# Row sums of the attention weights with queries on partitions, their reciprocals on VectorE, in a decoder layer on one core

## Chip, cores and metric

The kernel runs on 1 core of one Trainium2 chip. The metric is device time in microseconds, the median of three runs. One launch computes the whole layer: an attention with distance weights, a cross attention, and a mixture of experts.

## What is computed

Only the first of the three parts is touched. For each of 2 batches and 16 heads, with 1024 tokens and 64 columns per head (cut to what matters):

```python
P = X @ W_in + b_in                                  # X is the normalised input
Q, K, V, G = jnp.split(P, splits, axis=-1)
W = jnp.power(EPS + _cdist(Q, K), -P_POW)            # EPS = 1e-4, P_POW = 2
W = W / (EPS + jnp.sum(W, axis=-1, keepdims=True))   # the row sums
A = jnp.einsum('hbts,hbse->hbte', W, V)
H = G * A
return H @ W_out + b_out
```

The cross attention and the experts follow on `x + attention`.

## The kernel before, in words

The attention goes through 16 **pairs** of two heads (8 pairs for each batch). Weights of a pair lie in `wts` as [128 keys, head, 8 blocks of keys, 1024 queries]: keys on partitions, queries in the free dimension. The engines run one software pipeline that is written out by hand; each engine has its own program and waits on counting semaphores. In pair p:

- **TensorE** goes through 8 blocks of keys. Block b has `values(p, b)` (weights times V into `ps_o`, L593), a slice of `project_qk(p + 2)` (L488 into `ps_p`, from block 1 on), and `distances(p + 1, b)` (L577 into `ps_s`). `ps_s` has room for one block, so each `distances` waits until VectorE has taken the block before it. After the blocks come `project_v` and `project_g` of the next pair (L488), `turn_v` (8 transposes, L552), `row_sums(p)` (L606) and `norm_k(p + 2)` (L523, 8 matmuls of 2 columns).
- **VectorE** adds the first two blocks of weights into `acc_w` (`add_first`, L1027), and then has for each block `guard` (distances out of PSUM into `wts`, L1046) and `add_second` (the second head's sum, L1035). In between are the copies of q and k. The end of the pair has `copy_values`, `copy_vt`, `step_k`, `split_high`, `copy_v`, `split_low` (L1020 to L997), `copy_k2` (L1001) and `copy_g` (L1010). The first `distances` of the next pair waits for the last two.
- **ScalarE** takes the square roots of the next pair (`roots`, L1580), and then logarithm and exponential of the blocks (`weights`, L1586 and L1588), which give distance to the power of -2.
- **GpSimd** adds the first head's blocks (`add_block`, L1782) and splits weight matrices for the projections.

**Row sums before.** `acc_w` holds, for each head, the sum over the blocks, still with 128 keys on partitions. `row_sums` multiplies by a matrix of ones with 64 columns, so that `ps_p` gets the row sum of every query on the 64 partitions of its head: 4 matmuls of 512 columns. ScalarE takes `rinv = exp(-ln(sum + eps))` in two passes over 1024 columns (`rows_log` L1568, `rows_inverse` L1572), put between the chunks of the next pair's `weights`. GpSimd multiplies G by it (`gate_rows`, L1788), and VectorE multiplies the values by that product (`gate`, L1064).

In the last pair there is nothing to prepare, and TensorE runs `context()` ahead of the values: keys and values of the cross attention (L471 and L479, 80 records of few columns). VectorE has its own `context()` behind `add_first`. After the last pair, SyncE loads the input again, the output weights (both into the room of `wts`) and the first tile of heads, and TensorE begins `attn_out` (L666).

Of the kernel before, what the change touches and what calls it, by code (L numbers as in the profile page):

```python
# [108 lines left out]
def program(nc, x, ctx_t, mask, w_in, b_in, w_out, w_x, b_cols, rows_in, gate_w, w1, w2, w3, consts, r_consts, out):  # L109
    with ExitStack() as ctx:  # L110
# [46 lines left out]
        rinv = sb("rinv", [P, T])  # L157
        q32, k32, v_t = qk, norms, qk_sq
# [83 lines left out]
        def h_part(j, n):  # L242
# [42 lines left out]
                 "v_ok", "max_ok", "h_ok", "sqq_ok", "sqk_ok", "add0_ok", "add_ok", "addb_ok", "gr_ok", "sqrt_ok", "ln_ok", "w_ok", "rln_ok", "r_ok", "h_out",  # L285
# [161 lines left out]
        def _(pe):  # L447
# [45 lines left out]
            def project_qk(p, i0, i1, rows_before):  # L493
                for i in range(i0, i1):
                    if i == 0:
                        pe.wait_ge(S_.wqk_ok, 2 * p + 2)
                        if isinstance(p, int) and p == 1:
                            pe.wait_ge(S_.vt_ok, 1)
                        if rows_before is not None:
                            pe.wait_ge(S_.rln_ok, rows_before)  # L500
                    if i == STEPS:
                        pe.wait_ge(S_.q_ok, p + 1)
                    mm = project_step(ps_p, wqk_hi, wqk_lo, p, i // STEPS, i % STEPS)
                    if i == STEPS - 1:
# [91 lines left out]
            def row_sums(n, turned):  # L596
                pe.wait_ge(S_.add_ok, NA * (n + 1))
                pe.wait_ge(S_.addb_ok, NA * (n + 1))
                if turned:
                    pe.wait_ge(S_.vt_ok, n + 2)  # L600
                else:
                    pe.wait_ge(S_.rln_ok, n)
                for th in range(2):
                    t = slice(th * HALF, (th + 1) * HALF)
                    for h in range(2):
                        mm = pe.matmul(ps_p[h * DH:(h + 1) * DH, t], cst[:, C_ONES:C_ONES + DH], acc_w[:, h, t], start=True, stop=True)  # L606
                mm.then_inc(S_.sum_mm, 1)

            def pair(p, first=False, ahead=2):

                if ahead == 0:
                    context()
                for b in range(SB):
                    values(p, b)
                    if ahead == 2:
                        project_qk(p + 2, QK_STEPS[b], QK_STEPS[b + 1], None if first else p)
                    if ahead >= 1:
                        distances(p + 1, b)
                if ahead >= 1:
                    if ahead == 1:  # L620
                        pe.wait_ge(S_.rln_ok, p)
                    project_v(p + 1, p + 3 if ahead == 2 else PAIRS)
                    project_g(p + 1, ps_s[:, 1])
                    turn_v(p + 1)
                row_sums(p, ahead >= 1)
                if ahead == 2:
                    norm_k(p + 2, ps_s[:, 0])
# [25 lines left out]
            pair(PAIRS - 1, ahead=0)  # L653

# [48 lines left out]
            def turn_p(i, g, n):  # L703
                if g <= 1:
                    pe.wait_ge(S_.exp_ok, 3 * i + 2 + g)
                if g == 0:
                    if n == 0:
                        pe.wait_ge(S_.rln_ok, PAIRS)
# [208 lines left out]
        def _(dve):  # L917
# [141 lines left out]

            def gate(n):  # L1060
# [38 lines left out]
            def pair(p, first=False, ahead=2):  # L1099

                if ahead >= 1:
# [23 lines left out]
                if ahead == 2:  # L1125
                    split_low(p + 2)
                    copy_k2(p + 2)
                if ahead >= 1:
                    copy_g(p + 1)

# [32 lines left out]
            pair(PAIRS - 1, ahead=0)  # L1163
            dve.wait_ge(S_.x2_in, 16)
# [373 lines left out]
        def _(act):  # L1538
# [25 lines left out]
            def rows_log(n):  # L1564
                act.wait_ge(S_.sum_mm, n + 1)
                if not (isinstance(n, int) and n == 0):
                    act.wait_ge(S_.gr_ok, n)
                act.activation(rinv[:], ps_p[:], ACT.Ln, bias=eps_d[:, 0:1]).then_inc(S_.rln_ok, 1)  # L1568

            def rows_inverse(n):  # L1570
                act.wait_ge(S_.rln_ok, n + 1)
                act.activation(rinv[:], rinv[:], ACT.Exp, scale=-1.0).then_inc(S_.r_ok, 1)  # L1572

# [8 lines left out]
            def weights(n, first):  # L1582
                act.preload_act_table_set("natural_log_exp_and_others")  # L1583
                for c, (start, end) in enumerate(LOGS):
# [153 lines left out]
        def _(pool):  # L1738
# [85 lines left out]
            gate_rows(PAIRS - 1)  # L1824
# [122 lines left out]
```

## Time and profile before

| what | value |
|---|---|
| median of 3 runs | 1432.39 us (1429.56 to 1433.23) |
| the profiled execution: its own time | 1428.5 us |
| its span | 1426.4 us |
| TensorE busy | 1263.9 us, 89% |
| VectorE busy | 1132.7 us, 79% |
| ScalarE busy | 1036.4 us, 73% |
| GpSimd busy | 708.7 us, 50% |
| ScalarE, logarithm and exponential of the weights (L1586, L1588) | 246.0 and 238.4 us |
| VectorE, guards (L1046) | 296.9 us |

The busy time of an engine is the sum over its instructions, and engines overlap. The attention fills the first 22 of the page's 40 slices, about 800 us. In nearly all of these ScalarE and TensorE stand at 9 tenths or more, so the average over the whole span says little: what a change in the attention is worth is read from one of its pairs.

### The profile page before, as it was taken

What the parts mean: (1) busy time and instruction counts of PE and PEld (TensorE: products, weight loads), DVE (VectorE), ACT (ScalarE), POOL (GpSimd) and SP (SyncE); (2) the same over time, 40 slices, a digit from 0 to 9 for tenths busy, and PEclk for the clock granted to TensorE, in tenths of its full rate; (3) what the DMA queues carried; (4) which work ended last, traced back from release to release, by engine and by line L of the source; (5) the groups of instructions that cost most, each with busy time, mean ns of one, the idle gap of its engine ahead of it and who ended that gap; (6) DMA issues with size and microseconds to landing.
All of it is one profiled execution on the core that took longest, in us unless ns stands there. A gap on an engine that the chain in (4) does not pass through costs nothing.

```text
span 1426.4 us, 23505 instructions
## 1 busy us (share of the span) xinstructions
PE 1263.9 (89%) x7513; PEld 865.1 (61%) x7513; DVE 1132.7 (79%) x1569; ACT 1036.4 (73%) x839; POOL 708.7 (50%) x524
## 2 busy tenths in 40 slices
PE   5899999999999999999998955999993699999992
PEld 4545554554455455545544714888873599999992
DVE  7988998898889889888988473788886867777771
ACT  1699999999999999999999931333332356666661
POOL 5456656665665666566655152333330245565642
PEclk9999999999999999999999767999995799999996
DMA  5000000000000000000000124222220134334422
GB/s 156 5 11 16 30 15 29 15 22 22 15 29 15 29 15 29 15 29 15 15 22 0 28 76 130 85 67 66 66 98 15 31 91 123 76 97 98 101 30 74
DMA packets 69214, 67.78 MB, mean 48 GB/s; under 512 B 6816, under 2 KB 61600, under 8 KB 69152
## 3 DMA queue, kind: packets, MB, share of 16 engines
q1 hardware_dynamic: 61504, 56.91, 12.6%
q0 software_dynamic: 7680, 10.49, 4.4%
q8 instruction: 17, 0.28, 0.1%
q14 instruction: 13, 0.11, 0.0%
HBM read 49.29 MB, written 20.19 MB: 49 GB/s over the span
## 4 chain that ended last, share of the span: by engine, by line
PE 35%; ACT 19%; issue 19%; DVE 13%; DMA 7%; POOL 5%; POOLq 1%; DVEq 0%; ACTq 0%; SPq 0%
ACT wts L1586 11%; PE ps_s L577 8%; DMA acc<-norms,tok_put 6%; PE ps_o L593 6%; PE ps_o L666 4%; ACT wts L1588 4%; DVE wts L1046 3%; PE ps_p L488 3%; PE ps_o L879 2%; PE ps_s L699 2%; PE ps_s L727 2%; PE ps_s L846 2%; POOL head_rows L1864 2%; ACT L1583 1%; POOL tok_now L1861 1%
## 5 line engine op out<-in xcount | busy, mean ns | idle before, releaser
L1782 POOL TENSOR_TENSOR v_aug<-v_aug,wts 128x1024 f32<-128x1024 f32 x96 | 232.4, 2421 | 227.3 <-DVE v_aug L1035 226.9
L1046 DVE TENSOR_SCALAR wts<-ps_s,k 128x1024 f32<-128x1024 f32 x240 | 296.9, 1278 | 55.3 <-PE ps_s L577 51.9
L593 PE MATMUL ps_o<-wts,head_rows 128*64 128x512 f32 x1024 | 249.0, 610 | 3.6 <-ACT wts L1588 3.6
L1586 ACT ACTIVATE wts<-wts,eps_d 128x2048 f32<-128x2048 f32 (+1 forms) x96 | 246.0, 2562 | 0.2
L1580 ACT ACTIVATE wts<-wts 128x4096 f32<-128x4096 f32 (+1 forms) x80 | 230.1, 2931 | 21.0 <-DVE wts L1054 18.6
L1588 ACT ACTIVATE wts<-wts 128x2048 f32<-128x2048 f32 (+1 forms) x96 | 238.4, 2483 | 3.0
L577 PE MATMUL ps_s<-q_hi,k_hi 64*128 64x512 f32 x512 | 122.5, 471 | 34.0 <-DVE wts L1046 17.8
L593 PEld LDWEIGHTS ps_o<-wts,head_rows 128*64 128x64 f32 x1024 | 63.2, 137 | 128.0 <-issue 118.0
L1035 DVE TENSOR_TENSOR v_aug<-v_aug,wts 128x1024 f32<-128x1024 f32 x96 | 126.5, 1317 | 6.6 <-ACT wts L1588 6.2
L577 PEld LDWEIGHTS ps_s<-q_hi,k_hi 64*128 64x128 f32 x512 | 49.3, 185 | 103.4 <-DVE wts L1046 62.5
L577 PE MATMUL ps_s<-q_lo,k_hi 64*128 64x512 f32 x512 | 102.6, 392 | 0.0
L577 PE MATMUL ps_s<-q_hi,k_lo 64*128 64x512 f32 x512 | 102.5, 391 | 0.0
L846 PE MATMUL ps_s<-q_hi,xn_hi 128*128 (+1 forms) x320 | 93.1, 291 | 1.5 <-DVE q_lo L1481 1.5
L846 PE MATMUL ps_s<-q_hi,xn_lo 128*128 (+1 forms) x320 | 91.4, 286 | 0.0
L846 PE MATMUL ps_s<-q_lo,xn_hi 128*128 (+1 forms) x320 | 91.3, 285 | 0.0
L666 PE MATMUL ps_o<-wts,head_rows 128*128 128x256 f32 x256 | 78.2, 406 | 13.6 <-DMA head_rows<-h_t 13.6
L1637 ACT ACTIVATE v_aug<-v_aug 128x462 f32<-128x462 f32 (+1 forms) x48 | 26.2, 547 | 87.7 <-POOL v_aug L1837 86.7
L1881 POOL DMA_INDIRECT acc<-norms,tok_put x40 | 69.4, 1735 | 31.9 <-POOL tok_put L1878 25.7
L1694 ACT ACTIVATE norms<-ps_o,w_slot 128x256 f32<-128x256 f32 x40 | 17.5, 472 | 90.3 <-PE ps_o L879 77.0
L1837 POOL TENSOR_TENSOR v_aug<-v_aug,lmax 128x462 f32<-128x462 f32 (+1 forms) x48 | 41.2, 872 | 65.8 <-DVE lmax L1223 65.8
L1767 POOL TENSOR_TENSOR qk_sq<-head_rows 128x1024 f32<-128x1024 f32 x15 | 31.1, 2072 | 81.1 <-PE ps_o L552 73.7
L1464 DVE TENSOR_TENSOR xn_lo<-wts,xn_hi 128x1024 fp32r<-128x1024 f32 (+1 forms) x80 | 68.9, 884 | 1.2 <-issue 0.9
(280 smaller groups left out, 3170.7 us busy)
## 6 DMA issues: line engine op xcount, KB each, us to landing
wts<-in_w SPq DMA_DIRECT2D x16, 704.0 KB, 5.5
raw<-in_w_in SPq DMA_DIRECT2D x64, 128.0 KB, 2.3
h_t<-o_step SPq DMA_DIRECT2D x16, 512.0 KB, 2.7
head_rows<-h_t SPq DMA_DIRECT2D x16, 512.0 KB, 4.4
wts<-in_w SPq DMA_DIRECT2D x8, 640.0 KB, 7.5
acc<-wts SPq DMA_DIRECT2D x17, 128.0 KB, 1.8
wts<-in_x SPq DMA_DIRECT2D x2, 1024.0 KB, 5.9
wts<-in_x SPq DMA_DIRECT2D x1, 2048.0 KB, 9.2
```

The costliest lines, as they stand in the source:

```text
L577: mm = pe.matmul(ps_s[:, h, t], k[r], q[r, t], start=b == i == 0, stop=i == len(terms) - 1, skip_group_check=b > 0)
L593: mm = pe.matmul(ps_o[r, t], v_pair[:, b, r], wts[:, h, b, t], start=b == 0, stop=b == SB - 1)
L666: mm = pe.matmul(bank_a[:, 0:D], h_tile[:, par, q, :], w_o[:, q, :], start=q == 0, stop=q == H // 2 - 1)
L846: mm = pe.matmul(out, w, y_part, start=n == c == 0, stop=n == 2 and c == DC - 1)
L1035: dve.tensor_tensor(acc_w[:, 1], acc_w[:, 1], wts[:, 1, b], ALU.add).then_inc(S_.addb_ok, 1)
L1046: dve.tensor_scalar(wts[:, h, b, :], ps_s[:, h, :], k2[:, 2 * b + h:2 * b + h + 1], 0.0, ALU.add, ALU.max).then_inc(S_.max_ok, 1)
L1464: low = dve.tensor_tensor(lo, raw12, hi.bitcast(F32), ALU.subtract)
L1580: act.activation(chunk(start, end), chunk(start, end), ACT.Sqrt).then_inc(S_.sqrt_ok, 1)
L1586: act.activation(chunk(start, end), chunk(start, end), ACT.Ln, bias=eps_d[:, 0:1]).then_inc(S_.ln_ok, 1)
L1588: act.activation(chunk(start, end), chunk(start, end), ACT.Exp, scale=-2.0).then_inc(S_.w_ok, 1)
L1782: pool.tensor_tensor(acc_w[:, 0], acc_w[:, 0], wts[:, 0, b], ALU.add).then_inc(S_.add_ok, 1)
L1881: pool.indirect_dma_start(out=acc, out_offset=bass.IndirectOffsetOnAxis(ap=tok_put[:, par:par + 1], axis=0), in_=o_sb[:, par], in_offset=None,
```

## The change

Row sums are made with the queries on partitions. `row_sums` now takes 128 queries of `acc_w` as the stationary operand and one column of ones as the moving one: 16 matmuls with one column of output each, into 16 columns of `ps_p`. VectorE adds eps to the 128 x 16, takes the reciprocal, and spreads each value over 64 columns of `rinv` (three instructions, each waiting for the one before). TensorE turns `rinv` back with 8 transposes (`turn_rows_inverse`), and VectorE multiplies G by what is then in `ps_p` (`gate_rows`, moved from GpSimd). ScalarE's two passes are gone.

```diff
+        r_sum = sb("r_sum", [P, NB])
+        r_inv = sb("r_inv", [P, NB])
...
                         if rows_before is not None:
-                            pe.wait_ge(S_.rln_ok, rows_before)
+                            pe.wait_ge(S_.gr_ok, rows_before)
...
                 else:
-                    pe.wait_ge(S_.rln_ok, n)
-                for th in range(2):
-                    t = slice(th * HALF, (th + 1) * HALF)
+                    pe.wait_ge(S_.gr_ok, n)
+                for b in range(SB):
                     for h in range(2):
-                        mm = pe.matmul(ps_p[h * DH:(h + 1) * DH, t], cst[:, C_ONES:C_ONES + DH], acc_w[:, h, t], start=True, stop=True)
+                        mm = pe.matmul(ps_p[:, 2 * b + h:2 * b + h + 1], acc_w[:, h, b * P:(b + 1) * P], cst[:, C_ONES:C_ONES + 1],
+                                       start=True, stop=True)
                 mm.then_inc(S_.sum_mm, 1)
+            def turn_rows_inverse(n):
+                pe.wait_ge(S_.ri_ok, n + 1)
+                for b in range(SB):
+                    mm = pe.transpose(ps_p[:, b * P:(b + 1) * P], rinv[:, b * P:(b + 1) * P], ident)
+                mm.then_inc(S_.rt_mm, 1)
...
                     values(p, b)
+                    if b == 0 and not first:
+                        turn_rows_inverse(p - 1)
...
             pair(PAIRS - 1, ahead=0)
+            turn_rows_inverse(PAIRS - 1)
...
+            def rows_inverse(n):
+                dve.wait_ge(S_.sum_mm, n + 1)
+                dve.tensor_scalar(r_sum[:], ps_p[:, 0:NB], EPS_D, None, ALU.add).then_inc(S_.re_ok, 1)
+                dve.wait_ge(S_.re_ok, 2 * n + 1)
+                dve.reciprocal(r_inv[:], r_sum[:]).then_inc(S_.re_ok, 1)
+                dve.wait_ge(S_.re_ok, 2 * n + 2)
+                if not (isinstance(n, int) and n == 0):
+                    dve.wait_ge(S_.rt_mm, n)
+                dve.tensor_copy(rinv[:].rearrange("p (b d) -> p b d", d=DH), r_inv[:].unsqueeze(2).broadcast_to([P, NB, DH])).then_inc(S_.ri_ok, 1)
+
+            def gate_rows(n):
+                dve.wait_ge(S_.rt_mm, n + 1)
+                dve.wait_ge(S_.g_ok, n + 1)
+                g = vg[:, bass.ds(n & 1, 1)].rearrange("p a t -> p (a t)")
+                dve.tensor_tensor(g, g, ps_p[:], ALU.mult).then_inc(S_.gr_ok, 1)
...
             def pair(p, first=False, ahead=2):
+                if not first:
+                    gate_rows(p - 1)
                 if ahead >= 1:
                     dve.wait_ge(S_.k2_ok, p + 2)
                 add_first(p)
...
                     split_low(p + 2)
-                    copy_k2(p + 2)
                 if ahead >= 1:
                     copy_g(p + 1)
+                rows_inverse(p)
+                if ahead == 2:
+                    copy_k2(p + 2)
...
             pair(PAIRS - 1, ahead=0)
+            gate_rows(PAIRS - 1)
             dve.wait_ge(S_.x2_in, 16)
...
-            def rows_log(n):
-                act.wait_ge(S_.sum_mm, n + 1)
-                if not (isinstance(n, int) and n == 0):
-                    act.wait_ge(S_.gr_ok, n)
-                act.activation(rinv[:], ps_p[:], ACT.Ln, bias=eps_d[:, 0:1]).then_inc(S_.rln_ok, 1)
-
-            def rows_inverse(n):
-                act.wait_ge(S_.rln_ok, n + 1)
-                act.activation(rinv[:], rinv[:], ACT.Exp, scale=-1.0).then_inc(S_.r_ok, 1)
...
-                    if c == 1 and not first:
-                        rows_log(n - 1)
-                    if c == 3 and not first:
-                        rows_inverse(n - 1)
...
-            def gate_rows(n):
-                pool.wait_ge(S_.r_ok, n + 1)
-                g = vg[:, bass.ds(n & 1, 1)].rearrange("p a t -> p (a t)")
-                pool.wait_ge(S_.g_ok, n + 1)
-                pool.tensor_tensor(g, g, rinv[:], ALU.mult).then_inc(S_.gr_ok, 1)
...
                 for b in range(2, SB):
-                    if b == 4 and not first:
-                        gate_rows(p - 1)
                     add_block(p, b)
```

**Where instructions move.** First TensorE at the turn from one pair to the next, in the loop, before the change. `ps_p<-v_aug,cst` are the row sums, `ps_s<-cst,k_sq` is `norm_k`, and `ps_o<-wts,head_rows` is the first `values` of the next pair.

```order
L552 MATMUL ps_o<-cst,qk_sq 128x128 [waits oraw_ok,vt_ok]
L552 MATMUL ps_o<-cst,qk_sq 128x128 x7
L597 REGISTER_ALU
L606 MATMUL ps_p<-v_aug,cst 64x512 [waits vt_ok,addb_ok,add_ok]
L606 MATMUL ps_p<-v_aug,cst 64x512 x3
L521 ISA [waits sqk_ok]
L523 MATMUL ps_s<-cst,k_sq 128x2 [waits max_ok]
L523 MATMUL ps_s<-cst,k_sq 128x2 x7
L650 REGISTER_ALU
L650 COMPARE_AND_BRANCH
L593 MATMUL ps_o<-wts,head_rows 64x512 [waits w_ok,v_ok]
L593 MATMUL ps_o<-wts,head_rows 64x512 x3
L577 MATMUL ps_s<-q_hi,k_hi 128x512 [waits vt_ok,k2_ok,g_ok,sqq_ok,split_ok]
```

The same place after the change:

```order
L554 MATMUL ps_o<-cst,qk_sq 128x128 [waits oraw_ok,vt_ok]
L554 MATMUL ps_o<-cst,qk_sq 128x128 x7
L599 REGISTER_ALU
L607 MATMUL ps_p<-cst,v_aug 128x1 [waits vt_ok,addb_ok,add_ok]
L607 MATMUL ps_p<-cst,v_aug 128x1 x15
L523 ISA [waits sqk_ok]
L525 MATMUL ps_s<-cst,k_sq 128x2 [waits max_ok]
L525 MATMUL ps_s<-cst,k_sq 128x2 x7
L660 REGISTER_ALU
L660 COMPARE_AND_BRANCH
L595 MATMUL ps_o<-wts,head_rows 64x512 [waits w_ok,v_ok]
L595 MATMUL ps_o<-wts,head_rows 64x512 x3
L614 MATMUL ps_p<-cst,rinv 128x128 [waits ri_ok]
L614 MATMUL ps_p<-cst,rinv 128x128 x7
L579 MATMUL ps_s<-q_hi,k_hi 128x512 [waits vt_ok,k2_ok,g_ok,sqq_ok,split_ok]
```

The row sums are 16 matmuls of one column in place of 4 of 512, and 8 transposes of `rinv`, with a wait for VectorE (`ri_ok`), stand between the first values and the first distances.

Next VectorE at the same turn, before. `vg<-ps_s,b_pair` is `copy_g`, and `k<-ps_s` is `copy_k2`.

```order
L997 TENSOR_TENSOR k_lo<-o_step,k_hi 128x1024
L1001 COPY k<-ps_s 128x16 [waits k2_mm]
L1010 REGISTER_ALU [waits g_proj]
L1010 ISA
L1010 TENSOR_SCALAR vg<-ps_s,b_pair 128x1024
L1160 REGISTER_ALU
L1160 COMPARE_AND_BRANCH
L1027 TENSOR_TENSOR v_aug<-wts 128x1024 [waits sum_mm,w_ok,k2_ok]
L1027 TENSOR_TENSOR v_aug<-wts 128x1024
L1046 TENSOR_SCALAR wts<-ps_s,k 128x1024 [waits s_ready,add0_ok]
```

And after:

```order
L1021 TENSOR_SCALAR vg<-ps_s,b_pair 128x1024
L1073 TENSOR_SCALAR r_sum<-ps_p 128x16 [waits sum_mm]
L1074 REGISTER_ALU
L1075 RECIPROCAL r_inv<-r_sum 128x16 [waits re_ok]
L1079 COPY rinv<-r_inv 128x1024 [waits rt_mm,re_ok]
L1012 COPY k<-ps_s 128x16 [waits k2_mm]
L1191 REGISTER_ALU
L1191 COMPARE_AND_BRANCH
L1085 TENSOR_TENSOR vg<-vg,ps_p 128x1024 [waits g_ok,rt_mm]
L1038 TENSOR_TENSOR v_aug<-wts 128x1024 [waits sum_mm,w_ok,k2_ok]
L1038 TENSOR_TENSOR v_aug<-wts 128x1024
L1057 TENSOR_SCALAR wts<-ps_s,k 128x1024 [waits s_ready,add0_ok]
```

Three instructions of `rows_inverse` stand ahead of `copy_k2`, and the multiplication by the turned reciprocals stands ahead of `add_first`, behind a wait for TensorE (`rt_mm`).

Last, VectorE at the turn into the last pair, after the change. `k_raw<-ps_s,b_qk_x` is the first instruction of VectorE's `context()` that reads what TensorE's `context()` made.

```order
L1021 TENSOR_SCALAR vg<-ps_s,b_pair 128x1024 [waits g_proj]
L1073 TENSOR_SCALAR r_sum<-ps_p 128x16 [waits sum_mm]
L1075 RECIPROCAL r_inv<-r_sum 128x16 [waits re_ok]
L1079 COPY rinv<-r_inv 128x1024 [waits rt_mm,re_ok]
L1085 TENSOR_TENSOR vg<-vg,ps_p 128x1024 [waits g_ok,rt_mm]
L1038 TENSOR_TENSOR v_aug<-wts 128x1024 [waits sum_mm,w_ok]
L1038 TENSOR_TENSOR v_aug<-wts 128x1024
L1095 TENSOR_SCALAR mask_f<-mask_i 128x154 [waits c_in]
L1100 TENSOR_SCALAR k_raw<-ps_s,b_qk_x 128x77 [waits kv_mm]
L1100 TENSOR_SCALAR k_raw<-ps_s,b_qk_x 128x77 x3
```

TensorE has in its program there the row sums, then the whole of `context()`, then these:

```order
L595 MATMUL ps_o<-wts,head_rows 64x512 [waits w_ok,v_ok]
L595 MATMUL ps_o<-wts,head_rows 64x512 x3
L614 MATMUL ps_p<-cst,rinv 128x128 [waits ri_ok]
L614 MATMUL ps_p<-cst,rinv 128x128 x7
L595 MATMUL ps_o<-wts,head_rows 64x512 [waits w_ok]
```

So `gate_rows(14)` on VectorE, which stands ahead of `add_first` and `context()`, waits for transposes that TensorE issues behind its own `context()`.

## Rows read from the trace of the kernel before

**Rows 1.** Busy time by engine in one pair of the loop, us; last clock, DMA, GB/s
```profile
357.19:406.16 48.97, 47.05 (x250) 25.04 (x249) 43.65 (x39) 48.68 (x21) 29.74 (x17) 1.00 0.06 21
```

**Rows 2.** Timeline of ScalarE in that pair: start us, us, engine, line, instruction
```profile
366.18 1.10 ACT L1568 ACTIVATE rinv<-ps_p,eps_d 128x1024 f32<-128x1024 f32 x1
...
374.86 1.04 ACT L1572 ACTIVATE rinv<-rinv 128x1024 f32<-128x1024 f32 x1
```

**Rows 3.** Timeline of TensorE at the end of that pair and the start of the next
```profile
407.55 1.03 PE L552 MATMUL ps_o<-cst,qk_sq 128*128 128x128 f32 x8
408.51 1.94 PE L606 MATMUL ps_p<-v_aug,cst 128*64 128x512 f32 x8
410.38 1.95 PE L523 MATMUL ps_s<-cst,k_sq 128*128 128x2 f32 x16
412.26 1.94 PE L593 MATMUL ps_o<-wts,head_rows 128*64 128x512 f32 x8
414.85 0.50 PE L577 MATMUL ps_s<-q_hi,k_hi 64*128 64x512 f32 x2 [0.66 <-DVE vg L1010]
```

**Rows 4.** Timeline of VectorE over the same turn of the pair
```profile
408.36 0.69 DVE L992 CAST k_hi<-o_step 128x1024 fp32r<-128x1024 f32 x1
...
413.44 1.27 DVE L1010 TENSOR_SCALAR vg<-ps_s,b_pair 128x1024 f32 x1
415.28 2.78 DVE L1027 TENSOR_TENSOR v_aug<-wts 128x1024 f32<-128x1024 f32 x2 [0.57 <-ACT wts L1588]
```

**Rows 5.** Group of VectorE by line: the nearest reciprocal (busy us, mean ns)
```profile
L1241 DVE RECIPROCAL den<-ps_s 128x16 f32<-128x16 f32 x16 | 4.0, 248 | 0.6 <-PE ps_s L727 0.6
```

**Rows 6.** Timeline of TensorE, first distances of pair 0 and of pair 1
```profile
72.37 0.50 PE L577 MATMUL ps_s<-q_hi,k_hi 64*128 64x512 f32 x2 [1.00 <-DVE k_lo L997]
...
120.95 0.50 PE L577 MATMUL ps_s<-q_hi,k_hi 64*128 64x512 f32 x2 [0.95 <-DVE vg L1010]
```

**Rows 7.** Timeline of VectorE before pair 0, with GpSimd at work beside it
```profile
67.06 1.10 DVE L992 CAST k_hi<-o_step 128x1024 fp32r<-128x1024 f32 x1
```

**Rows 8.** Windows of 2 us with a change of clock (PE, PEld, DVE, ACT, POOL; PEclk)
```profile
30.00:32.00 2.00, 0.85 (x4) 0.81 (x6) 2.00 (x3) 0.00 (x0) 2.00 (x2) 0.64 0.00 0
32.00:34.00 2.00, 2.00 (x10) 1.17 (x8) 0.20 (x1) 0.00 (x0) 2.00 (x3) 0.51 0.55 152
804.00:806.00 2.00, 2.00 (x18) 2.00 (x17) 0.00 (x0) 1.97 (x2) 0.00 (x0) 0.85 0.00 0
824.00:826.00 2.00, 2.00 (x8) 0.66 (x6) 2.00 (x16) 2.00 (x2) 0.00 (x0) 0.53 0.00 0
838.00:840.00 2.00, 0.00 (x0) 0.00 (x0) 1.46 (x1) 0.00 (x0) 2.00 (x2) 0.88 0.00 0
```

**Rows 9.** Timeline of TensorE in the preparation
```profile
26.02 1.95 PE L523 MATMUL ps_o<-cst,k_sq 128*128 128x2 f32 x16 [0.70 <-POOL k_sq L1773]
31.15 0.80 PE L577 MATMUL ps_s<-q_hi,k_hi 64*128 64x512 f32 x2 [3.19 <-DVE k L1001]
```

**Rows 10.** Timeline of TensorE in the last two pairs
```profile
802.90 1.98 PE L471 MATMUL ps_s<-norms,w_x_sb 128*128 128x77 f32 x16 [0.73 <-DVE vg L1010]
804.72 15.95 PE L479 MATMUL ps_s<-w_x_sb,norms 128*128 128x32 f32 x80
820.59 16.55 PE L593 MATMUL ps_o<-wts,head_rows 128*64 128x512 f32 x64
```

**Rows 11.** Timelines of VectorE and GpSimd in the last two pairs
```profile
775.09 1.22 DVE L1035 TENSOR_TENSOR v_aug<-v_aug,wts 128x1024 f32<-128x1024 f32 x1 [2.76 <-ACT wts L1588]
...
820.70 0.91 DVE L1073 TENSOR_SCALAR k_raw<-ps_s,b_qk_x 128x77 f32<-128x77 f32 x4 [10.90 <-PE ps_s L479]
...
830.35 9.11 DVE L1035 TENSOR_TENSOR v_aug<-v_aug,wts 128x1024 f32<-128x1024 f32 x4
...
838.34 3.31 POOL L1788 TENSOR_TENSOR vg<-vg,rinv 128x1024 f32<-128x1024 f32 x1
...
848.49 5.83 POOL L1782 TENSOR_TENSOR v_aug<-v_aug,wts 128x1024 f32<-128x1024 f32 x2 [1.25 <-DVE v_aug L1035]
```

More of the change, by code:

```diff
@@ L284, in program @@
                  "v_turned", "s_ready", "av_blk", "sum_mm", "q_ok", "k_cp", "vt_ok", "g_ok", "hi_ok", "split_ok", "step_ok", "k2_ok",
-                 "v_ok", "max_ok", "h_ok", "sqq_ok", "sqk_ok", "add0_ok", "add_ok", "addb_ok", "gr_ok", "sqrt_ok", "ln_ok", "w_ok", "rln_ok", "r_ok", "h_out",
+                 "v_ok", "max_ok", "h_ok", "sqq_ok", "sqk_ok", "add0_ok", "add_ok", "addb_ok", "gr_ok", "sqrt_ok", "ln_ok", "w_ok", "re_ok", "ri_ok", "rt_mm", "h_out",
                  "eps_ok", "oraw_ok", "wo_in", "bp_ok",
@@ L620, in pair @@
                     if ahead == 1:
-                        pe.wait_ge(S_.rln_ok, p)
+                        pe.wait_ge(S_.gr_ok, p)
                     project_v(p + 1, p + 3 if ahead == 2 else PAIRS)
@@ L707, in turn_p @@
                     if n == 0:
-                        pe.wait_ge(S_.rln_ok, PAIRS)
+                        pe.wait_ge(S_.gr_ok, PAIRS)
                 if n >= 1 or g == 2:
@@ L1580, in roots, with weights @@
                     act.activation(chunk(start, end), chunk(start, end), ACT.Sqrt).then_inc(S_.sqrt_ok, 1)
-            def weights(n, first):
+            def weights(n):
                 act.preload_act_table_set("natural_log_exp_and_others")
@@ L1588, in weights @@
                     act.activation(chunk(start, end), chunk(start, end), ACT.Exp, scale=-2.0).then_inc(S_.w_ok, 1)
-                    if c == 1 and not first:
-                        rows_log(n - 1)
-                    if c == 3 and not first:
-                        rows_inverse(n - 1)
             roots(0)
-            weights(0, True)
+            weights(0)
             with act.Fori(1, PAIRS) as p:
                 roots(p)
-                weights(p, False)
-            rows_log(PAIRS - 1)
-            rows_inverse(PAIRS - 1)
+                weights(p)
             def probs_t(i, g, n):
@@ L1782, in add_block, with pair @@
                 pool.tensor_tensor(acc_w[:, 0], acc_w[:, 0], wts[:, 0, b], ALU.add).then_inc(S_.add_ok, 1)
-            def gate_rows(n):
-                pool.wait_ge(S_.r_ok, n + 1)
-                g = vg[:, bass.ds(n & 1, 1)].rearrange("p a t -> p (a t)")
-                pool.wait_ge(S_.g_ok, n + 1)
-                pool.tensor_tensor(g, g, rinv[:], ALU.mult).then_inc(S_.gr_ok, 1)
-            def pair(p, first=False, ahead=2, later=3):
+            def pair(p, ahead=2, later=3):
                 for b in range(2, SB):
-                    if b == 4 and not first:
-                        gate_rows(p - 1)
                     add_block(p, b)
@@ L1817, in _ @@
             split_vg(1)
-            pair(0, first=True)
-            with pool.Fori(1, PAIRS - 3) as p:
+            with pool.Fori(0, PAIRS - 3) as p:
                 pair(p)
@@ L1823, in _ @@
             pair(PAIRS - 1, ahead=0)
-            gate_rows(PAIRS - 1)
             pool.wait_ge(S_.gr_ok, PAIRS)
```

## Prediction

> **What bounds the kernel now.** I read the windows of one pair of the loop first. One pair takes 48.97 us; ScalarE is busy for 48.68 of them, TensorE for 47.05, VectorE for 43.65, GpSimd for 29.74, with TensorE at its full clock, 2.4 GHz [rows 1]. So ScalarE has no slack, and the change takes work from it. But TensorE lacks only 1.9 us of being as full, and most of that is waiting for VectorE. The timelines of the two engines at the turn of a pair say how they are tied: turn_v at 407.55, row sums 408.51, norm_k 410.38, values 412.26 to 414.13, and then the first distances at 414.85, which had waited 0.66 us for VectorE's copy_g [rows 3], begun at 413.44 and 1.27 long [rows 4]. There is also a pair that shows what ScalarE's relief alone is worth: pair 0 has no row logarithm or exponential on ScalarE, and from its first distances (72.37) to those of pair 1 (120.95) go 48.58 us [rows 6], against 48.97. The two bounds lie 0.4 us apart.
>
> **The change, part by part, at full clock.** Durations are those of the profiled execution.
>
> ScalarE loses 1.10 and 1.04 us per pair [rows 2], about 1.95 from start to start. By rows 6 that gives back 0.4 us a pair and no more, since the loop of TensorE and VectorE holds the rest.
>
> Row sums: 4 matmuls of 512 columns (8 records in the profile) took 1.87 us, 408.51 to 410.38 [rows 3]. The new 16 have 128 x 128 stationary operands and one column. Their nearest relative is norm_k: 8 such matmuls with two columns are 16 records in 1.88 us, 0.117 each [rows 3]. So 32 records by 0.117 = 3.75 us, 1.87 more on TensorE. Upwards it could be the 0.20 of L479 (80 records in 15.9 us [rows 10]), downwards nothing cheaper than 1.87 for the whole, the old price.
>
> The Trainium skill (TensorE: Matmul & The Clock Gate, Back-to-back issue gap) says that issue never drops below about 25 ns however few the columns. By that floor the 32 records would be an estimated 0.8 us instead of 3.75. The trace has 117 ns for two columns, since a load of weights goes with each, so I keep the row.
>
> Rows inverse on VectorE: an addition and a reciprocal on 16 columns, at most 0.25 us each by the reciprocal of the same shape [rows 5], and a spreading copy of 1024 columns within SBUF. A cast of that size took 0.69 alone [rows 4] and 1.10 with GpSimd at work beside it [rows 7]; GpSimd splits weights at this point, so 1.0. Together about 1.5, from copy_g's end at 414.7 to 416.2. TensorE, later by 1.87, is free at 416.0. The two paths end together, so only the longer counts: the transposes start at 416.3.
>
> The transposes are 8 like turn_v's, 0.96 us [rows 3], on the path: the first distances move from 414.85 to about 417.2, by 2.35. gate_rows, 1.2 us on VectorE, comes behind them, and add_first (2.78 [rows 4]) behind that, so the first guard is late and holds the second distances for about 0.2. Less the 0.4 of ScalarE's relief and a little of GpSimd's lighter load: **2.0 us more for each turn of the pair, at full clock**. GpSimd's own gate_rows goes from an engine with 19 us to spare and gives nothing in the loop.
>
> **The clock.** Row sums and norm_k now stand together: 3.75 + 1.88 = 5.6 us in which TensorE loads weights and sends one or two columns. What thin work does to the clock is in the trace. TensorE's dense work ended at 802.2; L471 and L479, with 77 and 32 columns or so a record, followed, and the granted clock fell from 2.4 to 1.2 GHz at 805.4 (a mean of 0.85 over 804 to 806, between 1.00 and 0.50) and stayed there, although matmul and weight load were both busy all of the time, until 825.9, 5.3 us after values had begun again at 820.6 [rows 8, 10]. It fell 2.4 us after the last value of 837.1, at 839.5 [rows 8, 10]. In the preparation it fell at 30.6, 5.3 us after the projections had ended at 25.3, with norm_k in between, and came back at 34.0, 2.8 us after 31.2 [rows 8, 9]. So it falls 2.4 to 5.3 us after the dense work ends and returns 2.8 to 5.3 us after it begins again. With norm_k alone, 1.9 us, it held 1.00 in the loop [rows 1].
>
> I therefore expect a fall in nearly every turn: midway between these, about 3.9 us into the 5.6, so that 1.7 us of thin work run at 0.20 instead of 0.117 us a record (1.2 us more), and then 4.0 us of values, transposes and distances at half speed (2.0 us lost). That is 3.2 us a turn; between 0.2 + 1.4 = 1.6 (late fall, quick return) and 2.3 + 2.6 = 4.9.
>
> The same page of the Trainium skill (The HAM clock gate) counts the ramp as under 1% of a typical span and advises not to model more. By that the clock would cost an estimated 14 us at most in the whole kernel, where my rows give 45; it is a rival below.
>
> **The end of the attention.** Pair 14 loses a wait: VectorE stood 2.76 us for ScalarE's weights at 775.09 [rows 11], and with 1.95 less work there and a later start it will not. I take 2 us back.
>
> Then comes the largest single step. TensorE issues transposes for pair 14 behind its own context() and one values, and VectorE has gate_rows, add_first and its context() behind them. Before, VectorE's context began at 820.70 [rows 11]. Now TensorE's context ends 1.1 later (1.87 more, less the 0.73 it waited [rows 10]), 821.7; the first values at half clock are 3.7, the transposes about 1.9, gate_rows 1.2, add_first 2.4: 831. That is 10.3 late, and the adds behind context, from 830.35, move by as much. They get back 2: GpSimd's gate_rows of 3.31 no longer stands among its adds [rows 11]. GpSimd's last two adds (848.49, 5.83 [rows 11]) end about 8.2 later, and with them move the loads that wait for them. The last row sums, at 1.2 GHz, take 32 by 0.20 = 6.4, then VectorE and the turn back, some 3.5 more, where the old ones ended well before the first tile landed: 1.2 more. Tail: 9.4.
>
> **Sum.** 14 turns (after pairs 0 to 13) by 2.0 + 3.2 = 73, less 2, plus 9.4: **+80 us**. The profiled execution took 1428.5 (span 1426.4), so 1508.5. It lay 3.9 below the median of the runs, so the median should be about **1512 us**.
>
> **Rivals.**
> - *The clock holds.* Weight loads might count as work, or the fall come too late for 5.6 us. For: norm_k alone never lowered it. Against: L479 kept it low for 20 us with weight loads back to back. 14 by 2.0, less 2, plus 9.4 = +35: 1468. By the page's 1%, +49: 1481. Together 0.14.
> - *The sums are dearer*: 0.20 a record at full clock, 2.7 us more a turn, and a longer stretch at half clock: about +120, 1552. Nothing loads that slowly at 2.4 GHz in rows 3. 0.05.
> - *Faster than before.* ScalarE's chain is the true bound, and VectorE and TensorE hide inverse and turn in their waits. The loop would then go at ScalarE's 48.97 - 1.95 = 47.0: 13 by -1.95, plus 9.4, gives 1416. It needs the path through copy_g, inverse, transposes and distances to grow by less than 0.4 us a turn, the gap of rows 6, with no fall of the clock; I find 2.35. 0.04.
> - *No difference*: a small loss in the turns paid for by ScalarE. It needs the same path to grow by no more than about 0.3, and most of the tail to vanish. 0.02.
> - *Forecast*, falls in most turns: 0.75.
>
> **Range.** Low and high of the forecast are 14 by 3.6 + 7.4 = +58 (1490) and 14 by 6.9 + 7.4 = +104 (1536). For 8 in 10 I take the high end as it stands and go down to the case in which the clock holds: 1466 to 1534. A measurement of this kernel tells about 0.3% (4 us) from no change; slower by more than that has 0.94, within it 0.02, faster 0.04.
>
> **What would show it.** Right: row sums of 32 records and about 3.75 us where the clock is full; PEclk below 1.00 in windows of a loop pair; first distances 5 us later after turn_v; ScalarE idle 5 us or more a pair, behind guards; transposes of pair 14 after 823, and VectorE's context behind them. Wrong: PEclk 1.00 through the loop (then 51 us a pair), records of the sums well off 0.117, or a VectorE context that begins with TensorE's end.

## The result, and the profile after

The changed kernel takes **1514.44 us** (median of 4 runs, 1509.86 to 1518.28), the kernel before 1432.08 (1429.56 to 1433.23): a ratio of 1.0576, 95% interval 1.054 to 1.0613. The forecast was 1512 in a range of 1466 to 1534. The profiled execution took 1509.86 us, with a span of 1508.0; forecast was 1508.5 for its own time.

The page of the changed kernel, engines and the chain that ended last by engine:

```profile
PE 1354.2 (90%) x8025; PEld 954.5 (63%) x8025; DVE 1163.6 (77%) x1633; ACT 1008.6 (67%) x807; POOL 655.0 (43%) x508
...
PE 61%; DVE 15%; issue 10%; DMA 7%; POOL 4%; ACT 1%; DVEq 1%; POOLq 1%; ACTq 0%; SPq 0%
```

In the chain ScalarE has 1% where it had 19%, and TensorE 61% where it had 35%. ScalarE is out of the way, and TensorE has the largest share of the chain. One pair of the loop, from its first distances to the next (columns as in [rows 1], whose pair took 48.97 us):

```profile
341.24:393.55 52.31, 51.27 (x282) 29.03 (x282) 45.52 (x42) 45.51 (x19) 25.63 (x16) 0.97 0.06 19
393.55:447.43 53.88, 52.78 (x281) 30.41 (x280) 45.51 (x42) 48.53 (x21) 25.96 (x17) 0.94 0.06 20
```

TensorE now has 1.0 to 1.1 us to spare in a pair, with a granted clock of 0.94 or 0.97. The pairs differ in length although they do the same work; the difference is the clock. The turn that ends the second of them, on TensorE, answers to [rows 3]:

```profile
435.08 1.03 PE L554 MATMUL ps_o<-cst,qk_sq 128*128 128x128 f32 x8
435.95 3.63 PE L607 MATMUL ps_p<-cst,v_aug 128*128 128x1 f32 x32
439.44 2.67 PE L525 MATMUL ps_s<-cst,k_sq 128*128 128x2 f32 x16
442.04 3.68 PE L595 MATMUL ps_o<-wts,head_rows 128*64 128x512 f32 x8
445.66 1.85 PE L614 MATMUL ps_p<-cst,rinv 128*128 128x128 f32 x8
447.43 0.50 PE L579 MATMUL ps_s<-q_hi,k_hi 64*128 64x512 f32 x2
```

and the clock over it, in windows of 2 us (columns as in [rows 8]):

```profile
438.00:440.00 2.00, 2.00 (x20) 2.00 (x20) 2.00 (x2) 2.00 (x2) 2.00 (x3) 1.00 0.00 0
440.00:442.00 2.00, 2.00 (x13) 2.00 (x12) 2.00 (x2) 1.97 (x2) 1.92 (x2) 0.61 0.00 0
442.00:444.00 2.00, 2.00 (x7) 0.75 (x9) 1.49 (x5) 2.00 (x2) 2.00 (x4) 0.50 0.00 0
444.00:446.00 2.00, 2.00 (x8) 0.39 (x5) 0.00 (x0) 1.97 (x2) 1.92 (x3) 0.50 0.45 131
446.00:448.00 2.00, 2.00 (x12) 1.71 (x12) 0.20 (x1) 2.00 (x2) 0.02 (x1) 0.69 0.24 70
```

In this turn the sums run at full clock, 32 records from start to start in 3.49 us, 0.109 each. The clock falls from 2.4 to 1.2 GHz within norm_k, at 440.4 (0.61 over 440 to 442 is 0.44 us at 1.00 and the rest at 0.50), and is back at 447.2. In between norm_k takes 2.67 instead of 1.95, the values 3.68 instead of 1.94, the transposes 1.85 instead of 1.03. VectorE is not what holds the transposes:

```profile
440.88 1.27 DVE L1021 TENSOR_SCALAR vg<-ps_s,b_pair 128x1024 f32 x1
442.08 0.16 DVE L1073 TENSOR_SCALAR r_sum<-ps_p 128x16 f32<-128x16 f32 x1
442.27 0.25 DVE L1075 RECIPROCAL r_inv<-r_sum 128x16 f32<-128x16 f32 x1
442.56 0.92 DVE L1079 COPY rinv<-r_inv 128x1024 f32<-128x1024 f32 x1
...
447.80 1.22 DVE L1085 TENSOR_TENSOR vg<-vg,ps_p 128x1024 f32 x1 [4.23 <-PE ps_p L614]
```

Addition, reciprocal and spreading copy take 1.40 us from 442.08 to the end of the copy at 443.48; then gate_rows waits 4.23 us for the turned reciprocals. ScalarE, which was full, now waits for the guards (here in one pair):

```profile
370.93 3.63 ACT L1602 ACTIVATE wts<-wts 128x4096 f32<-128x4096 f32 x1 [3.58 <-DVE wts L1057]
...
379.45 1.92 ACT L1602 ACTIVATE wts<-wts 128x2048 f32<-128x2048 f32 x1 [2.31 <-DVE wts L1057]
```

**Where the 81.6 us of the span went.** The first distances of pair 0 start 0.72 later (73.09). From there to the first distances of pair 14 the loop needs 752.53 us (to 825.62) where it needed 685.41 (72.37 to 757.78): 67.1 for 14 turns, 4.79 a turn. From turn_v to the first distances a turn takes 10.75 us in 3 turns, 12.1 to 12.4 in 9 and 14.0 in 2, where the turn of [rows 3] took 7.3. The clock fell in each of the 14. From the first distances of pair 14 to the end of the attention stage 8.9 more, and the stages behind it, which the change doesn't touch, 4.9 more. That last term is not the change's: from the end of the attention (the first `k_sq<-wts,ps_o` on VectorE) to the end of the span the twelve profiled runs of this study took 552.4 to 562.7 us, all with the same code there; the kernel before took 557.9, the changed one 562.7 and, in a second profile, 557.5.

The end of the attention on TensorE and VectorE:

```profile
869.63 2.88 PE L473 MATMUL ps_s<-norms,w_x_sb 128*128 128x77 f32 x16
872.31 16.56 PE L481 MATMUL ps_s<-w_x_sb,norms 128*128 128x32 f32 x80
888.80 3.68 PE L595 MATMUL ps_o<-wts,head_rows 128*64 128x512 f32 x8
892.41 1.97 PE L614 MATMUL ps_p<-cst,rinv 128*128 128x128 f32 x8
...
929.32 6.99 PE L607 MATMUL ps_p<-cst,v_aug 128*128 128x1 f32 x32 [22.75 <-POOL v_aug L1798]
```

```profile
894.42 1.22 DVE L1085 TENSOR_TENSOR vg<-vg,ps_p 128x1024 f32<-128x1024 f32 x1 [23.22 <-PE ps_p L614]
...
897.98 0.90 DVE L1100 TENSOR_SCALAR k_raw<-ps_s,b_qk_x 128x77 f32<-128x77 f32 x4
...
907.60 9.11 DVE L1046 TENSOR_TENSOR v_aug<-v_aug,wts 128x1024 f32<-128x1024 f32 x4
```

From TensorE's context to VectorE's context it was 17.80 us (802.90 to 820.70, [rows 10, 11]); now 28.35 (869.63 to 897.98), with VectorE idle for 23.22 ahead of gate_rows.

### The profile page after: what moved, and what is told of

Read it like the earlier page. It is cut to its first block, busy times and chain, and to the rows that moved or that the text cites. A ratio compares the mean times of both kernels' runs of the same rounds, so it can differ in the third digit from the quotient of the medians.

```text
span 1508.0 us, 24547 instructions
## 1 busy us (share of the span) xinstructions
PE 1354.2 (90%) x8025; PEld 954.5 (63%) x8025; DVE 1163.6 (77%) x1633; ACT 1008.6 (67%) x807; POOL 655.0 (43%) x508
## 4 chain that ended last, share of the span: by engine, by line
PE 61%; DVE 15%; issue 10%; DMA 7%; POOL 4%; ACT 1%; DVEq 1%; POOLq 1%; ACTq 0%; SPq 0%
PE ps_o L595 13%; PE ps_s L579 11%; PE ps_p L490 8%; DMA acc<-norms,tok_put 6%; PE ps_p L607 4%; PE ps_o L677 3%; DVE wts L1057 3%; PE ps_s L490 3%; PE ps_s L525 2%; PE ps_o L890 2%; PE ps_s L710 2%; PE ps_s L738 2%; DVE v_aug L1038 2%; DVE v_aug L1046 2%; PE ps_s L857 2%
## 5 line engine op out<-in xcount | busy, mean ns | idle before, releaser
L1602 ACT ACTIVATE wts<-wts 128x4096 f32<-128x4096 f32 (+1 forms) x80 | 233.6, 2938 | 110.9 <-DVE wts L1057 92.0
L595 PE MATMUL ps_o<-wts,head_rows 128*64 128x512 f32 x1024 | 274.0, 662 | 1.4 <-ACT wts L1610 1.4
L595 PEld LDWEIGHTS ps_o<-wts,head_rows 128*64 128x64 f32 x1024 | 67.2, 146 | 133.2 <-issue 125.8
L607 PE MATMUL ps_p<-cst,v_aug 128*128 128x1 f32 x512 | 63.5, 258 | 22.8 <-POOL v_aug L1798 22.8
L1085 DVE TENSOR_TENSOR vg<-vg,ps_p 128x1024 f32 (+1 forms) x16 | 19.5, 1222 | 80.2 <-PE ps_p L614 80.2
L607 PEld LDWEIGHTS ps_p<-cst,v_aug 128*128 128x128 f32 x512 | 63.7, 206 | 23.6 <-POOL v_aug L1798 23.6
```

What stands on the lines that cost most here:

```text
L595: mm = pe.matmul(ps_o[r, t], v_pair[:, b, r], wts[:, h, b, t], start=b == 0, stop=b == SB - 1)
L607: mm = pe.matmul(ps_p[:, 2 * b + h:2 * b + h + 1], acc_w[:, h, b * P:(b + 1) * P], cst[:, C_ONES:C_ONES + 1], start=True, stop=True)
L1602: act.activation(chunk(start, end), chunk(start, end), ACT.Sqrt).then_inc(S_.sqrt_ok, 1)
```

## The experiments

The theory of the prediction: the turn of a pair, TensorE's and VectorE's path through the inverse together, grew by about 2 us at full clock; on top the clock falls in each turn, because sums and norm_k stand as one stretch of thin matmuls; and at the end VectorE's context stands behind the late transposes. Rivals: thin matmuls are merely slow, and the clock plays no part; or the length of the turn comes from VectorE or the order alone. Ten experiments ran (one is the changed kernel once more), in three groups, each on one chip with the kernel before beside it (medians of 1429.38, 1428.58 and 1430.95 us there). A **turn from turn_v** is the stretch from the transposes of turn_v to the first distances of the next pair; a turn of the loop is a whole pair, from first distances to first distances. A matmul is called thin when it has one or two columns of output, dense when it has 512. The medians are of 4 runs (5 for the small passes).

### Dense matmuls in place of the thin ones

`e1_dense_same_length` takes the changed kernel with the old matmuls, issued twice, in all 16 pairs:

```
-  for b in range(SB):
-      for h in range(2):
-          pe.matmul(ps_p[:, 2*b+h : 2*b+h+1], acc_w[:, h, b*P:(b+1)*P], cst[ones, 1 column])
+  for _ in range(2):
+      for th in range(2):
+          for h in range(2):
+              pe.matmul(ps_p[h*DH:(h+1)*DH, t], cst[ones, DH columns], acc_w[:, h, t])
```

> The changed kernel with its 16 one-column matmuls of the row sums replaced by the old four of 512 columns, issued twice. TensorE spends the same 3.75 us there, but on dense work. VectorE goes on reading 16 columns of what they leave, so the normalisation is no longer by the row sums (left out of the computation); everything else is as in the change. My theory (thin work lowers the clock, about 3 us a turn): the granted clock stays at 1.00 through the loop, the turn from turn_v to the first distances falls from 12.3 to about 9.3 us, a pair takes about 51 us, and the time is 1465 to 1472. Rival (the length of the sums and the new waits cost the time, the clock only reports it): within 10 us of the changed kernel, 1505 to 1515.

It took 1458.56 us (1457.67 to 1460.99), ratio 1.0212 (1.0195 to 1.0229). The clock and one turn:

```profile
60.00:788.00 728.00, 707.34 (x3739) 374.52 (x3737) 648.58 (x599) 672.25 (x275) 370.31 (x229) 1.00 0.06 19
```

```profile
371.46 3.65 PE L609 MATMUL ps_p<-v_aug,cst 128*64 128x512 f32 x16
375.05 1.95 PE L525 MATMUL ps_s<-cst,k_sq 128*128 128x2 f32 x16
376.92 1.94 PE L595 MATMUL ps_o<-wts,head_rows 128*64 128x512 f32 x8
378.96 1.09 PE L615 MATMUL ps_p<-cst,rinv 128*128 128x128 f32 x8
379.99 0.51 PE L579 MATMUL ps_s<-q_hi,k_hi 64*128 64x512 f32 x2
```

The sums take as long as the thin ones, 3.65 us, and everything behind them is in the same order; but the clock stays at 2.4 GHz, a turn from turn_v takes 9.48 us instead of 10.75 to 14.0, and the loop's turns 51.02 on average ((788.24 - 74.00) / 14) instead of 53.75. The turn is as expected, the whole 6 us below the expected band; the end of the attention, below, has its part in that. So of the 4.79 us a turn, 2.06 are length at full clock and 2.73 go with the fall of the clock. The dense matmuls differ from the thin ones in more than their columns: they are 16 records in place of 32, with the matrix of ones as the stationary operand (64 columns) in place of the weights' sums (128). Which of these lets the clock fall was not separated.

`e2_dense_half_length` issues the old matmuls once (`for _ in range(1)`).

> The same with the old four matmuls issued once, 1.87 us in place of 3.75 (row sums left out likewise). My theory: the clock holds and VectorE's path (copy of g, inverse, spreading copy) is about as long as TensorE's, so that taking 1.87 us from TensorE wins less than 0.7 us a turn: 1458 to 1468, at most 10 below the dense run of full length. Rival (TensorE's path alone decides): 1.87 by 14 = 26 us below it, about 1442.

It took 1462.55 us (1460.18 to 1463.65), ratio 1.023 (1.0212 to 1.0247); the loop's turns are 51.03 again but for the first (51.81) and one of 52.40 in which the clock fell, at 686, although no thin matmul but norm_k's stood in it. With 1.8 us less on TensorE nothing is gained:

```profile
375.56 1.94 PE L595 MATMUL ps_o<-wts,head_rows 128*64 128x512 f32 x8
379.27 1.09 PE L615 MATMUL ps_p<-cst,rinv 128*128 128x128 f32 x8 [1.77 <-DVE rinv L1080]
```

```profile
376.63 1.27 DVE L1022 TENSOR_SCALAR vg<-ps_s,b_pair 128x1024 f32 x1
...
378.30 0.91 DVE L1080 COPY rinv<-r_inv 128x1024 f32<-128x1024 f32 x1
```

TensorE now waits 1.77 us for rinv, which VectorE makes only behind copy_g. The two paths end together, each good for 51.0. In this run the sums are done at about 373.7, before copy_g begins at 376.63, so VectorE does not wait for them, and even free row sums would not give the 2 us back. That the place of the inverse in VectorE's order costs them, behind copy_g, is my reading; no run moved it alone.

### Thin and dense matmuls added to the kernel before

The reverse test: the kernel before, with the same extra time between its row sums and norm_k, once as 16 thin matmuls, once as 8 dense ones, into a PSUM bank that the next distances overwrite:

```
   row_sums(p, ...)
+  extra(p)      # e3: 16 of 128x1, 32 records; e4: 8 of 512 columns, 16 records
   norm_k(p + 2, ps_s[:, 0])
```

> The kernel before, untouched in ScalarE, VectorE and GpSimd, with 16 more one-column matmuls (results unused) between its row sums and norm_k in pairs 0 to 13, so that 5.6 us of thin work stand together. My theory: 3.1 us a turn for the work (3.75 less the 0.66 that TensorE waited) and about 3.2 for the clock: +43 and +45, 1515 to 1525, with half clock after each turn as in the changed kernel. Rival (the clock falls only with the changed kernel's waits): +43 alone, 1475.

> The kernel before with eight more matmuls of 512 columns (results unused) at the same place, 3.74 us of dense work in place of the thin. My theory: +3.1 us a turn and the clock at 1.00: 1472 to 1480, 35 to 50 us under its thin twin. Rival (dense and thin work of one length cost the same): equal to the thin twin within 8 us.

The thin ones gave 1505.35 us (1503.06 to 1506.75), ratio 1.0528 (1.0511 to 1.0546); the dense ones 1462.95 (1461.77 to 1464.62), ratio 1.0234 (1.0217 to 1.0251). Both are below their expectations by about ten (3.7 us of added dense work lengthened a turn by 2.4 us and not by 3.1), but 42.4 us apart. Thin first, then dense, TensorE and clock:

```profile
60.00:840.00 780.00, 761.87 (x3960) 425.72 (x3960) 619.70 (x546) 701.21 (x304) 395.38 (x242) 0.93 0.05 18
```

```profile
60.00:790.00 730.00, 712.89 (x3728) 369.13 (x3724) 623.59 (x542) 694.18 (x300) 407.67 (x242) 1.00 0.06 19
```

TensorE is as busy in the one as in the other (98%), and its weight loads are busier in the kernel whose clock falls (425.72 of 780 against 369.13 of 730). The turns are 54.75 and 51.33 us: the clock costs 3.4 a turn here, in a kernel that has neither the inverse on VectorE nor the transposes. Thin matmuls added alone bring it.

### Fewer thin matmuls

`e10_half_the_sums` leaves every second half of the blocks out in the loop (`range(SB // 2)`).

> The changed kernel with 8 of the 16 sums left out in the loop's turns (the other 8 columns keep what stands there), so the thin stretch is 1.87 us shorter. If the clock falls by the amount of thin work: no falls; VectorE's path then decides as with the four dense matmuls, 51.0 us a turn, 1460 to 1465. If the norms and the turning back alone were enough: falls as before, 52 to 53 us a turn, 1485 to 1500.

It took 1478.24 us (1474.40 to 1481.03), ratio 1.0341 (1.0319 to 1.0363), between the two expectations. A turn:

```profile
377.12 1.84 PE L607 MATMUL ps_p<-cst,v_aug 128*128 128x1 f32 x16
378.83 1.93 PE L525 MATMUL ps_s<-cst,k_sq 128*128 128x2 f32 x16
380.69 3.46 PE L595 MATMUL ps_o<-wts,head_rows 128*64 128x512 f32 x8
384.69 1.09 PE L614 MATMUL ps_p<-cst,rinv 128*128 128x128 f32 x8 [0.54 <-DVE rinv L1079]
385.71 0.50 PE L579 MATMUL ps_s<-q_hi,k_hi 64*128 64x512 f32 x2
```

The clock still falls in each turn. Here it does so at 381.0, where the thin stretch of 3.6 us has already ended; only the values run at half speed (3.46 instead of 1.94). And that is nearly free: TensorE would have waited for rinv anyway, 1.77 us in the run with the dense matmuls issued once, 0.54 here. Six of the 14 turns last 51.0 us as if nothing had happened; in the others the half clock began earlier or lasted longer, and the mean is 51.78. The first expectation had "no falls" wrong and the 51.0 right; what a fall costs depends on what stands behind it.

### The same thin matmuls, spread out

`e7_spread_thin_work` and `e9_spread_behind_values` build on the kernel of the next section and put denser work between the thin matmuls. Core of the second (in the first, six blocks of sums stand within and right behind project_v, the last two behind turn_v within project_g, and VectorE's inverse ahead of copy_k2 and copy_g):

```
-  project_v; project_g; turn_v; row_sums; norm_k
+  project_v; project_g[0:3]; sums[0:2]; project_g[3:6]; sums[2:4]
+  project_g[6:9]; sums[4:6]; project_g[9:]; turn_v; sums[6:8]; norm_k[0:4]
+  # norm_k[4:8] between the halves of values(p, 0)
```

> The kernel of the run before this one, with the same thin matmuls of each turn spread out: the 16 sums two to four at a time between the projections' steps, the norms' 8 matmuls in two halves, nothing removed. If TensorE's clock falls because the thin matmuls stand together in one stretch: no or few falls in the loop, turns of 50.5 to 51.5 us as with the dense matmuls, 1450 to 1462 us. If their mere number does it: a fall in each turn, 53 to 54 us a turn, 1495 to 1510. Slower than the kernel before in both.

> The spread kernel again without its two side effects: the projection of the values is left whole, so that VectorE starts its turn as early as in the changed kernel, and VectorE's order is the changed kernel's. The 16 sums stand in pairs of blocks between the steps of the gate's projection and behind the turned values, the norms in two halves around half a block of values. TensorE's waits of 0.6 to 0.8 us in the turn go. If waits were part of what let the clock fall: fewer falls than in the first spread kernel (9 or 10 of 14), turns of about 51.3 us, 1455 to 1470. If it is the amount of thin work, in whatever order: a fall in most turns, 53 to 54 us, 1490 to 1505.

The first took 1512.53 us (1509.26 to 1514.61), ratio 1.0587 (1.0562 to 1.0612). That is above both expected bands. The clock held in 5 of its 14 turns, but these took 52.6 to 53.7 us. I put that down to the sums within project_v, which make VectorE's turn begin late; TensorE then waits for it:

```profile
124.76 1.09 PE L636 MATMUL ps_p<-cst,rinv 128*128 128x128 f32 x8 [0.79 <-DVE rinv L1113]
126.12 0.50 PE L585 MATMUL ps_s<-q_hi,k_hi 64*128 64x512 f32 x2 [0.27 <-DVE vg L1055]
```

The second took 1521.25 us (1518.5 to 1522.75), ratio 1.0639 (1.062 to 1.0658): again above both bands, with a fall in each turn, 54.94 us a turn. My expectation that its waits would go was wrong: sums ahead of turn_v delay the turned values, VectorE idles for them, and the transposes wait longer than before:

```profile
447.63 1.04 PE L560 MATMUL ps_o<-cst,qk_sq 128*128 128x128 f32 x8
...
455.91 1.97 PE L636 MATMUL ps_p<-cst,rinv 128*128 128x128 f32 x8 [1.57 <-DVE rinv L1112]
```

```profile
448.71 1.23 DVE L1058 COPY head_rows<-ps_o 128x1024 f32<-128x1024 f32 x1 [2.25 <-PE ps_o L560]
```

So these two ways of spreading did not save the clock: with the thin matmuls in groups of four between 512-column ones it still fell in 9 turns of 14, and with a group of eight behind turn_v (four sums, four norms) in all 14. Why the first kept it in 5 turns is open.

### What ScalarE's relief was worth

`e5_before_small_passes` is the kernel before with ScalarE's two passes of the loop made passes over one column: an exponential of a constant in place of the logarithm, which no longer reads `ps_p`, and an exponential into one column of `rinv`.

> The kernel before, with ScalarE's two passes over 128x1024 (logarithm and exponential of the row sums) made passes over one column in the 13 turns of the loop; the row normalisation is thereby left out. If ScalarE only keeps pace with the others, as the prediction's 0.4 us of relief per turn has it: 13 x 0.4 = about 5 us less, 1424 to 1428 us. If ScalarE truly sets the turn: its two passes less two short ones, 1.7 to 1.9 us a turn, 22 to 25 us less, 1404 to 1408. If the relief is nothing: 1429 to 1432.

It took 1422.54 us (1417.37 to 1426.62), beside 1428.58 for the kernel before on that chip, ratio 0.9956 (0.9932 to 0.9981). In the profiled run the turns take 48.62 us ((754.35 - 73.69) / 14) instead of 48.96. With ScalarE's 2 us nearly gone the gain is 0.34 us a turn, and the whole lies 1.5 us below the lowest expectation: ScalarE was full, but not alone.

### The end of the attention

`e6_turn_ahead_of_context` is the changed kernel with one call moved, in the last pair only:

```
   if ahead == 0:
+      turn_rows_inverse(p - 1)
       context()
   for b in range(SB):
       values(p, b)
-      if b == 0 and not first:
+      if b == 0 and not first and ahead:
           turn_rows_inverse(p - 1)
```

> The changed kernel, with TensorE's turning back of pair 14's reciprocals issued ahead of its context block instead of behind it. If VectorE's wait for it, 23.22 us before gate_rows in the last pair, is what makes the context start late: context on VectorE some 5.7 us earlier against the last distances, the run about 5 to 6 us faster than the changed kernel (ratio to before about 1.053 to 1.054). If the last pair is bound elsewhere (GpSimd's adds or the half clock of the context block): no difference beyond 1 us.

> The changed kernel once more, on the chip of the three runs beside it, as their reference: 1510 to 1518 us, a fall of the clock in each of the 14 turns.

The moved version took 1498.86 us (1498.24 to 1504.76), ratio 1.0498 (1.0466 to 1.0531), the changed kernel on the same chip 1504.90 (1500.27 to 1510.86), ratio 1.0543 (1.0503 to 1.0582). The repeated kernel came out 5 us below its expected band, with the clock falling in each of the 14 turns as expected; its ratio's interval overlaps that of the result. VectorE in the moved version:

```profile
870.62 1.22 DVE L1086 TENSOR_TENSOR vg<-vg,ps_p 128x1024 f32<-128x1024 f32 x1 [2.06 <-PE ps_p L614]
871.76 2.35 DVE L1039 TENSOR_TENSOR v_aug<-wts 128x1024 f32<-128x1024 f32 x2
...
890.30 0.91 DVE L1101 TENSOR_SCALAR k_raw<-ps_s,b_qk_x 128x77 f32<-128x77 f32 x4 [16.04 <-PE ps_s L481]
```

gate_rows and add_first are done 16 us before the context needs VectorE, and the context starts 67.5 us after the first distances of pair 14 instead of 72.4 (in both runs of the change). The attention's end comes 4.8 us earlier against those distances (114.8 against 119.6), and the medians are 6.0 apart, though their intervals overlap. The traces show the step, worth about 5; the times agree with it but don't prove it. It is the fastest version that ran of those that compute the whole change, and still 5% slower than the kernel before. None was faster than that kernel except the one that leaves part of its work out, by 0.4%.

The dense run of the first experiment says something of this end too, for it has no thin sums ahead of TensorE's context. There the clock fell at 838.4, 6.0 us into the context; in the changed kernel it fell at 870.5, 0.9 us into it, and in the kernel before at 805.4, 2.5 us into it. The context's first group and VectorE's context in the dense run:

```profile
832.38 2.01 PE L473 MATMUL ps_s<-norms,w_x_sb 128*128 128x77 f32 x16
```

```profile
855.94 0.91 DVE L1101 TENSOR_SCALAR k_raw<-ps_s,b_qk_x 128x77 f32<-128x77 f32 x4
```

From TensorE's context to VectorE's it is 23.56 us there, against 28.35 in the change and 17.80 before. From the first distances of pair 14 to the end of the attention it is 113.6, against 119.6 and 110.7. But the reference moves too: three runs with the same code there as the kernel before (thin added, dense added, small passes) took 104.7, 107.9 and 106.4 us, and in them the clock fell 5.2 to 7.3 us into the context. So both the new order and the moment of the fall take part in the 8.9 us, 6.0 of them are gone with dense sums, and single microseconds of this end are not the change's.

## Why the prediction was right, point by point

- **Relief of ScalarE, 0.4 us a turn**: 0.34 by the small passes. Right. (TensorE lacked 1.6 us of being as full as ScalarE; the 1.9 of the prediction is its idle time in the pair.)
- **Row sums, 32 by 0.117 = 3.75**: 3.49 from start to start. The floor of 25 ns of the Trainium skill (TensorE: Matmul & The Clock Gate, Back-to-back issue gap) is not what sets this: the trace has a weight load for each record and shows 109 ns.
- **The inverse, 1.5 us, and the two paths ending together**: 1.40 us, and the dense matmuls at full and at half length gave the same 51.03. Right.
- **2.0 us a turn at full clock**: 2.06.
- **The fall of the clock in nearly every turn**: in each of the 14. **Its price, 3.2 us a turn**: 2.73 here, 3.4 when the thin matmuls were added to the kernel before. The working was off in two places that nearly cancel, which is luck. I had the fall 3.9 us into the thin stretch; in the turn shown it came 4.5 us in (435.95 to 440.4), in the turn before it not until the stretch had ended, and in the two longest turns 2.4 us in. So in most turns less thin work and more values ran slowly. And I let the half clock last 1.7 + 4.0 = 5.7 us, while it lasted about 3.4 us in three turns, 6.8 in nine and 10.2 in two. Loop in all: 67.1 measured, 73 predicted.
- **Pair 14 gives 2 back, the tail costs 9.4**, together 7.4: 8.9, but the agreement is in part luck. From the first distances of pair 14 to TensorE's context it became 1.1 us shorter (predicted 0.9: 2 back, 1.1 for the sums); from there to VectorE's context 10.5 longer. GpSimd's adds took back 2.3 (predicted 2) and the last sums and transposes cost 1.8 (predicted 1.2). The middle term was too small (I had 9.2), because I took TensorE's context over at its old length, 17.7 us to the first values. It took 19.2, at the half clock from 0.9 us behind its start (L473 2.88 us instead of 1.98). With dense sums ahead of it, it took 14.6, and the whole end became 2.9 longer instead of 8.9. The prediction had the order as the cause of the step; the moment at which the clock falls there has a part in it too, 4.8 us of the middle term between the change and the run with dense sums.
- **The sum, +80**: +81.6 in the span, of which 4.9 lie in untouched code. Without these the change would have been 76.7: loop 6 too high, start and tail 2.2 too low.
- **Rival, the clock holds (1468)**: refuted by the windows, and by the run with dense matmuls, which shows what that case would have been, 1458.56, 29 above the kernel before on its chip where I had 35 (its end grew by 2.9 and not by 7.4, and the untouched stages were 3.9 shorter). What the Trainium skill says (TensorE: Matmul & The Clock Gate, The HAM clock gate), that the ramp is under 1% of a span, is said of the ramp after a start; the prediction was wrong to stretch it to falls in the middle of the kernel. Here the clock fell again in each of 14 turns, and 38 us (14 by 2.73) are 2.5% of the span of 1508.0.
- **Rivals, dearer sums and ScalarE as the bound**: 0.109 us a record, and 0.34 us a turn; both refuted.

## What to carry to other kernels

An engine that is full in the windows is a bound only as far as the next one: before taking work off it, find a stretch that has that work missing already (here pair 0) and read what it saves. Moving a reduction to another layout adds a dependency that runs through two engines and a turn back; its cost is its place in the path, not its instructions. And many one-column matmuls between dense ones must be priced twice: for themselves, and for the half clock at which the dense work behind them may run (as in each of the 14 turns here), which only costs where TensorE is the later path.

## What the runs showed of the hardware that was not expected

- Replacing 3.65 us of 512-column matmuls by 3.63 us of one-column matmuls, with matmul and weight load both busy all the time, brings a fall from 2.4 to 1.2 GHz in each of 14 turns, where before there was none; and TensorE's busy share does not tell the kinds apart: 98% with added thin and with added dense matmuls, with the weight loads busier in the kernel whose clock fell.
- The fall can come after the thin work has ended, among dense matmuls: in the run with half the sums at 381.0, when the values had begun at 380.69.
- The same work had half clocks of different length from turn to turn (3.4, 6.8 and 10.2 us), worth 10.75, 12.3 and 14.0 us from turn_v to the first distances. The mix differs from run to run: the changed kernel's second profile had five turns of 10.75, eight of about 12.3 and one of 14.0, and its loop took 747.4 us instead of 752.5. This may be why runs of the changed kernel scatter more (8.4 us over four runs, against 3.7 before).
